# Masked attention on one Trainium2 core: the sums of each batch in two groups, each directly ahead of a set of scores

## The reference, cut to what matters

```python
H = 256
NH = 16
def attention(q, k, v, mask):
    scores = jnp.einsum('bhqd,bhkd->bhqk', q, k) / jnp.sqrt(jnp.float32(HD))
    scores = scores * mask - 10000.0 * (1.0 - mask)
    probs = jax.nn.softmax(scores, axis=-1)
    return jnp.einsum('bhqk,bhkd->bhqd', probs, v)
ln_out = layernorm(hidden_states, ln1_s, ln1_b)
qkv = ln_out @ w_qkv + b_qkv
...
x = hidden_states + attn_out
```

## Time and profile before

| | |
|---|---|
| median of 3 runs | 2290.07 us (2288.86 to 2290.38) |
| profiled execution, its own time | 2288.72 us |
| span of its instructions | 2287.0 us |
| granted clock of TensorE, mean | 0.975 of full speed |
| TensorE busy | 2163.2 us, 95% |
| ScalarE, VectorE, GpSimd busy | 1573.8, 1552.3, 725.3 us |

### The profile page before, as it was taken

How to read it: one execution, slowest core, us unless ns; L and a number is a source line. 1 busy time by engine, 2 the same in 40 slices (tenths; PEclk the granted TensorE clock), 3 DMA queues, 4 the chain that set the end, 5 groups by cost and what they waited for, 6 DMA issues and landing times. The chain is left out here.

```text
span 2287.0 us, 51191 instructions
## 1 busy us (share of the span) xinstructions
PE 2163.2 (95%) x17289; PEld 1757.5 (77%) x17289; DVE 1552.3 (68%) x3940; ACT 1573.8 (69%) x4479; POOL 725.3 (32%) x885
## 2 busy tenths in 40 slices
PE   6999999999999999997989999789999989899998
PEld 5899999998999999997975666456666679666664
DVE  5555555557555555557659999587776676799985
ACT  4666666665667666665737777577787776488875
POOL 2211111123211111102024655377777720233201
PEclk9999999999999999998979999799999999799999
DMA  5111012100110010002000000100000000000001
GB/s 134 24 24 24 24 24 61 25 24 1 24 24 24 24 24 24 1 1 72 2 8 11 11 9 6 39 8 2 6 15 17 14 8 5 7 10 11 7 4 38
DMA packets 72943, 47.11 MB, mean 21 GB/s; under 512 B 29232, under 2 KB 71601, under 8 KB 72753
## 3 DMA queue, kind: packets, MB, share of 16 engines
q1 hardware_dynamic: 71664, 43.57, 7.6%
q10 hardware_dynamic: 1088, 1.05, 0.1%
HBM read 41.45 MB, written 2.10 MB: 19 GB/s over the span
## 5 line engine op out<-in xcount | busy, mean ns | idle before, releaser
L2105 DVE TENSOR_REDUCE maxima<-bank 128x2 f32<-128x512 f32 x512 | 333.1, 682 | 33.1 <-PE bank L1084 30.4
L1667 ACT ACTIVATE probs_t<-bank 128x512 f32<-128x512 f32 x512 | 282.3, 601 | 65.4 <-PE bank L1075 64.0
L1961 DVE SCALAR_TENSOR_TENSOR wide_heads_low<-bank,wide_columns,wide_heads_high 128x128 fp32r<-128x128 f32 x512 | 155.9, 346 | 211.1 <-ACT wide_heads_high L1532 211.0
L1520 ACT ACTIVATE wide_probs<-bank,wide_neg_max 128x129 f32<-128x129 f32 x512 | 184.1, 365 | 119.4 <-DVE wide_neg_max L1941 114.9
L1515 ACT ACTIVATE wide_probs_t<-bank 128x256 f32<-128x256 f32 x256 | 98.5, 385 | 161.1 <-PE bank L946 159.0
L2462 POOL TENSOR_TENSOR wide_columns<-wide_pair_columns,zero 128x8 f32<-128x8 f32 x16 | 3.4, 211 | 646.3 <-DVE x L1974 638.6
L1945 DVE RECIPROCAL wide_inverse<-wide_sums 128x2 f32<-128x2 f32 x256 | 42.5, 166 | 227.5 <-ACT wide_probs L1520 227.5
L1526 ACT ACTIVATE wide_probs<-wide_probs,wide_inverse 128x128 f32<-128x128 f32 x448 | 156.2, 396 | 52.1 <-DVE wide_inverse L1945 52.1
L1084 PE MATMUL bank<-k_packed,q_packed 32*128 32x256 f32 x1024 | 174.7, 341 | 3.9 <-ACT q_packed L1652 2.2
L1075 PE MATMUL bank<-q_packed,k_packed 32*128 32x256 f32 x1024 | 168.3, 333 | 8.4 <-ACT probs_t L1667 7.7
L1704 ACT ACTIVATE probs<-scores_masked,neg_max 128x128 f32<-128x128 f32 x512 | 163.4, 394 | 11.0 <-DVE neg_max L2284 10.2
(11 more groups left out here) (315 smaller groups left out, 6754.5 us busy)
## 6 DMA issues: line engine op xcount, KB each, us to landing
cn<-in_ctx SPq DMA_DIRECT2D x48, 128.0 KB, 2.1
q_packed<-max_rows SPq DMA_DIRECT2D x256, 4.0 KB
wide_pair_weights<-in_L_xattn_wq SPq DMA_DIRECT2D x15, 256.0 KB, 2.8
wide_pair_weights<-in_L_xattn_wk SPq DMA_DIRECT2D x15, 256.0 KB, 3.1
wide_pair_weights<-in_L_xattn_wv SPq DMA_DIRECT2D x15, 256.0 KB, 3.6
wide_pair_weights<-in_L_xattn_wo SPq DMA_DIRECT2D x15, 256.0 KB, 3.3
x<-in_x SPq DMA_DIRECT2D x4, 512.0 KB, 7.3
wide_ctx_rows<-in_ctx SPq DMA_DIRECT2D x4, 512.0 KB, 7.9
```

The source lines that it names most:

```text
L1520: last = act.activation(probs0[:, b, h, :], wide_scores[b % 2][:, h * KEYS0:(h + 1) * KEYS0], ACT.Exp, bias=neg_max0[:, b, h:h + 1], accum ...
L1667: act.activation(probs_t[j % 8][:, :], shifted_bank[j % 2][:, :], ACT.Exp, bias=0.0).then_inc(s.exp_ready, 1)
L1961: last = dve.scalar_tensor_tensor(heads_low[:, h, a, :], wide_heads[a % 2][:, h * P:(h + 1) * P], columns[slot][:, 3, h:h + 1], heads_high ...
L2105: dve.tensor_reduce(maxima[pack // 2][:, b, pack % 2, :], head_scores[packed_scores(1 - u, j)][:, :].rearrange("p (a k) -> p a k", a=UNITS ...
```

## The change

The block that makes the sums moves from the middle of the step to its end. The sums of t = 0 and 1 stay at j = 1, but now stand behind the transposes of older sums, so directly ahead of the scores of j = 2. The sums of t = 2 and t = 3 leave j = 2 and the middle of j = 3, and stand together at the end of j = 3, directly ahead of the scores of the next window. All waits in the block stay with it.

```diff
--- before.py
+++ after.py
@@ -1293,15 +1293,6 @@
                         last.then_inc(s.result, 1)
                         if isinstance(n, int) and n == 2 * B + 1:
                             turn_hidden(ROUNDS)
-                    for t in (0, 1) if past and j == 1 else (j,) if past and j else ():
-                        pe.wait_ge(s.probs_copied, g - j + t - 3)
-                        if t == 0:
-                            pe.wait_ge(s.v_ready, n)
-                            after(pe, s.sums_copied, n - 1)
-                        for m in range(PACK):
-                            last = pe.matmul(sums2_bank[m * QUAD:(m + 1) * QUAD, t * P:(t + 1) * P], vn[1 - u][:, 0, PACK * t + m, :],
-                                             probs_t[t][:, m * P:(m + 1) * P], start=True, stop=True)
-                        last.then_inc(s.sums, 1)
                     if ahead and j == 0:
 
                         layer, b = ahead
@@ -1339,6 +1330,15 @@
                             for c in range(DC):
                                 pe.matmul(project2_bank[:, m * P:(m + 1) * P], w_qkv[:, layer, c, m * P:(m + 1) * P],
                                           rows_t[u][:, c, :], start=c == 0, stop=c == DC - 1)
+                    for t in (0, 1) if past and j == 1 else (2, 3) if past and j == 3 else ():
+                        pe.wait_ge(s.probs_copied, g - j + t - 3)
+                        if t == 0:
+                            pe.wait_ge(s.v_ready, n)
+                            after(pe, s.sums_copied, n - 1)
+                        for m in range(PACK):
+                            last = pe.matmul(sums2_bank[m * QUAD:(m + 1) * QUAD, t * P:(t + 1) * P], vn[1 - u][:, 0, PACK * t + m, :],
+                                             probs_t[t][:, m * P:(m + 1) * P], start=True, stop=True)
+                        last.then_inc(s.sums, 1)
 
             over_sequence(pe, window)
```

## The result

The changed kernel took 2295.64 us (median of 8 runs, 2292.11 to 2301.65), beside 2289.26 us of the kernel before (2286.54 to 2290.46). The ratio is 1.0027, with an interval from 1.0019 to 1.0036: slower by 0.27%, some 6 us. The prediction was 2293.2 us, in a range of 2288 to 2300. One timed run of the kernel before, of 8473 us, was in a slow state, and no figure here uses it.

A forecast was written before the change was run, and what follows sets the result against it. TensorE's order and gaps were taken to bound the kernel. Window terms -0.3 + 1.0 + 1.0 + 1.4 + 0.2 - 0.2 gave +3.1 us, so 2291.8 profiled and 2293.2 us as the median, range 2288 to 2300.

The forecast's parts named there:

- What bounds the stage: Masked stage: TensorE's order and its gaps set the pace; TensorE is busy for 47.98 of 50 us there.
- A change of shape: TensorE switching tile shape between neighbouring instructions: 0.10 us lost at the border, more in the first instruction behind it.
- Rival 2: Ahead of each set of scores, the direct change from sums is dear, up to 0.20 us; over 0.2% slower; chance 0.34.
- Half one: Window part from scores at j = 0 to scores at j = 2: 5.33 us, forecast to gain 0.15.
- half two: Window part from scores at j = 2 to the next window's scores: 5.76 us, forecast to get 0.11 us longer.
- The new wait: In half two, L1331 (L1322 in the changed kernel) must wait 0.4 us for VectorE's addition L2264.
- S2: Start of the scores at j = 2 in a window, the zero point for later times; 1609.93 us in n = 11.
- Rival 1: In half two the wait on L2264 does not bind; 0.64 us gained in 30 windows, 19 us, 2271; chance 0.08.
- The 0.09 us at the second transposes: In half two, the second L1268 waits 0.09 us for the turn bank to be given back, starting at S2 + 2.50.
- restarted L1322: Projection of values (old L1331) after its wait: taken as 0.89 us; a slow 0.96 would add 2.0 over 29 windows.
- The sum: Total of the window-by-window gains and losses over the masked stage: +3.1 us.
- within 0.2%: Whole-run verdict: a loss of zero to 4.6 us, up to 2294.7; chance 0.58.

The follow-up runs named there:

- e3: Changed kernel with the result product of j = 2 written to the half of bank 3 that the sums of t = 2 and 3 fill later; 2275.23 us, ratio 0.9940.
- e8: Kernel of e3 with the projection of keys moved ahead of the transposes of j = 1; 2264.24 us, ratio to before 0.9891.
- e6: Changed kernel with the sums of t = 2 and 3 directly ahead of the projection of values at j = 3; 2281.58 us, ratio to before 0.9961.
- e1: Kernel before with only the sums of t = 0 and 1 moved directly ahead of the scores of j = 2; 2287.77 us, ratio 0.9998.
- e5: Changed kernel with VectorE's addition to x moved ahead of its product for queries and keys; 2283.22 us, ratio to before 0.9966.
- e10: Changed kernel measured once more, with no further edit; 2296.38 us, ratio to before 1.0021.

## Why the prediction was right, step by step

- *What bounds the stage.* Right: TensorE's order and its waits. Where one wait went (e3, e8), the time fell by about the amount worked out (e3: the runs 14 us under before, where 12 was expected; e8: the stage 12.2 us shorter than in e3, where 12 was).
- *A change of shape costs 0.10 at the border and 0.05 or 0.10 behind it.* Right, for the direct change from sums to scores too (0.58 for 16 sums and the border, taken as 0.57). Rival 2, that this change is dear, is refuted by both places of the profile after. The Trainium skill, TensorEngine Tiling (Array Packing), Key Properties, says that such a change drains TensorE; the trace agrees, with that 0.10. But a count of drains does not give the time: ten before, six in the changed kernel and seven in e6 stand at 11.09, 11.13 and 10.75 us a window.
- *Half one gains 0.15.* Right to 0.01 (5.33 to 5.18), and e1 shows it alone. That even windows give it back holds only together with half two (e1 against the changed kernel).
- *The new wait.* Right: L2264 ends at S2 + 3.37 and L1322 starts at S2 + 3.42, as put down. e3 and e5 show that this wait is what keeps the gain away. Rival 1 said what would come without it, 0.64 a window and 19 us; without it (e3) a window is 11.09 - 10.56 = 0.53 shorter and the runs 14 us. The 0.09 us at the second transposes, which still wait for ScalarE, and their restart (0.02) are the difference in a window; the rest is in windows such as n = 4, which became only 0.42 shorter. I had seen nothing in the order that would let L2264 be earlier; e5 found one place for it and had half two at 5.62.
- *The size, the term that was off.* From L1322 to the scores I took 2.45 us, with 0.89 for the restarted L1322; it was 2.53, with 0.97 for it. I had named that as a bound (0.96, "+0.07 at 29 windows, +2.0") and taken the other end, from the transposes, which lose 0.02 by a restart. With 0.08 more most windows come to within 0.04 of what was measured: +0.04 in n = 11, +0.15 in n = 12, +0.57 in n = 4, +0.46 in n = 20, where I had -0.04, +0.10, +0.50 and +0.34. Only n = 3, 5 and 7 do not: they measured +0.09 each, near my +0.10, but by errors that cancel: half one kept its gain there (5.17), which I had put as lost, and half two grew by 0.25. The sum was +3.1, the stage shows +4.7. The rows of before already held the right size. In n = 4 the old L1331 restarts behind the same wait, and the next group stands 0.97 behind it, not 0.89:

```profile
1535.57 1.13 PE L1331 MATMUL bank<-w_qkv,rows_t 128*128 128x256 f32 x4 [0.50 <-DVE x L2264]
1536.54 1.05 PE L1340 MATMUL bank<-rows_t,w_qkv 128*128 128x128 f32 x8
```

So my 1.95 us "before" for this window had the slow restart in it and my 2.45 "after" did not; the difference had to be the 0.57 of the 16 sums, which is what n = 4 measured.
- *The verdict.* I gave most to "within 0.2%" (0.58) and 0.34 to slower. The point was right, 0.14% against 0.27% measured and 0.21% in the stage; the likelier side of the border was not. The 0.08 us of the restart alone, in 29 windows, moves the sum from +3.1 to +5.4, across that border of 4.6.

## What to carry to other kernels

Before work is moved behind a wait, look up when the wait's releaser is done: work that stood ahead of the wait cost nothing for as long as the releaser was not done. Here sums that ran under another engine's addition were put behind it, and six changes of shape with the wait were slower than ten without. A bank that two products share is an order between three engines; with one product in another bank the same order of TensorE gained 14 us, where without that it had lost 6. And measure a small change by the period of its own loop, where two profiles agree to 0.02 us in a steady window, before trusting whole runs that spread over 10 us, and compare the granted clocks of such runs.

## What the runs showed of the hardware

- The first 256-wide float32 product behind a wait in which TensorE stood idle loses some 0.11 us, also with no change of shape ahead of it: L1322 takes 0.97 us from start to start after the wait in the changed kernel (1615.46 to 1616.43) and 0.86 without one in e3 (1609.93 to 1610.79). A change of shape ahead of the wait adds nothing to it: 0.97 in n = 4 of before (1535.57 to 1536.54). The 128-wide transposes lose 0.02 to 0.03 (0.46 for four, 1607.10 to 1607.56 in before, against 0.44 in e8, 1610.51 to 1610.95).
- TensorE started 0.05 to 0.06 us behind the recorded end of the VectorE addition that released it, in the changed kernel (1615.41 to 1615.46) and in e5 (1615.09 to 1615.15).
- A change of shape costs about the same for every pair seen, 0.10 at the border: the eight instructions of a projection take 0.99 and not 0.89 ahead of 32-column sums and ahead of 64-row scores alike, and 16 sums take 0.57 ahead of the full array and 0.58 straight ahead of the scores.
- Whole runs of one kernel differ in time along with the mean granted clock, by some 1 us for each 0.001 (e10: 2286.69 us at 0.980, 2299.51 at 0.970).
